# Filler matmuls on TensorE in a fused attention and expert-layer kernel: between the last four pair tiles, in the first six steps of the second attention pass, and in the prologue

## What is computed

```python
# layer 1: causal attention, 16 heads of 8 features, one shared key and value head
x = x + softmax(mask(q @ k.T / sqrt(8))) @ v @ w_proj      # q, k, v from layernorm(x) @ w_attn
# layer 2: experts picked by product keys, 8 heads, 16 experts each
xn = rmsnorm(layernorm(x)) * gamma
sim = (xn @ wq.T) . keys              # two lists of 32 key scores for each head
top 16 of sx[i] + sy[j], softmax over them
h = gelu(xn . table_down[idx]) * softmax(scores)
x = x + sum(h * table_up[idx])
```

## Time and profile before

| what | value |
|---|---|
| median of 3 runs | 1240.45 us (1239.9 to 1243.85) |
| the profiled execution | 1239.02 us |
| its span | 1237.2 us (1.8 us of the time lie outside the span) |
| mean granted TensorE clock | 0.763 |
| TensorE matmul, VectorE, ScalarE, GpSimd busy | 75%, 75%, 58%, 53% of the span |

### The profile page before, as it was taken

How to read it: one execution, slowest core, us unless ns; L and a number is a source line. 1 busy time by engine, 2 the same in 40 slices (tenths; PEclk the granted TensorE clock), 3 DMA queues, 4 the chain that set the end, 5 groups by cost and what they waited for, 6 DMA issues and landing times.

```text
span 1237.2 us, 21178 instructions
## 1 busy us (share of the span) xinstructions
PE 923.1 (75%) x5537; PEld 486.3 (39%) x5554; DVE 927.3 (75%) x4050; ACT 722.8 (58%) x1008; POOL 654.8 (53%) x371
## 2 busy tenths in 40 slices
PE   2784869687786968688796968778696877878544
PEld 1431425334343533434353443435344344534333
DVE  1325396987959597795959779595977959598997
ACT  1342574756657574665757466565756657574742
POOL 1100183764918276492927548292755829274843
PEclk9985766868778686877868686877868687777777
DMA  5211111020112102011110202011110201100000
GB/s 142 31 14 30 14 30 15 8 39 0 33 13 33 14 11 35 0 34 13 33 14 14 32 0 37 9 33 14 20 26 0 40 7 29 15 9 2 5 1 9
DMA packets 51537, 26.50 MB, mean 21 GB/s; under 512 B 5168, under 2 KB 51120, under 8 KB 51312
## 3 DMA queue, kind: packets, MB, share of 16 engines
q1 hardware_dynamic: 51504, 26.11, 12.9%
HBM read 19.93 MB, written 5.24 MB: 20 GB/s over the span
## 4 chain that ended last, share of the span: by engine, by line
PE 50%; DVE 30%; issue 9%; ACT 7%; DMA 2%; SPq 1%; DVEq 1%; POOL 0%; ACTq 0%; POOLq 0%
DVE prob L906 12%; PE score L1103 8%; PE misc L1123 7%; PE score L1073 6%; PE score L1105 5%; PE score L1076 5%; DVE late_scores L773 5%; PE score L1196 4%; ACT prob L636 4%; PE score L1153 3%; PE score L1184 3%; PE misc L1125 2%; PE misc L1163 2%; DVE cand_left L870 2%; ACT late_scores L540 2%
## 5 line engine op out<-in xcount | busy, mean ns | idle before, releaser
L445 POOL TENSOR_TENSOR acc<-acc,prob 128x1024 f32<-128x1024 f32 x186 | 441.2, 2372 | 16.6 <-DVE prob L906 0.5
L906 DVE SCALAR_TENSOR_TENSOR prob<-score,cut,prob 128x1024 f32<-128x1024 f32 x256 | 316.4, 1278 | 26.2 <-ACT prob L636 25.0
L636 ACT ACTIVATE prob<-score,neg_lse,unit 128x1024 f32<-128x1024 f32 x256 | 299.5, 1201 | 56.3 <-PE score L1184 37.3
L1184 PE MATMUL score<-sel,pieces_t 128*128 128x512 f16 x512 | 172.7, 433 | 121.4 <-DVE prob L906 119.1
L418 POOL TENSOR_TENSOR scale<-bounded,half_neg 128x2 f32<-128x2 f32 x16 | 11.2, 703 | 375.3 <-DVE bounded L817 375.3
L557 ACT ACTIVATE probs<-score 128x512 f32<-128x512 f32 x192 | 114.7, 597 | 140.6 <-PE score L1105 120.0
L1103 PE MATMUL score<-q_stack,k_stack 49*128 49x512 bf16 x192 | 110.8, 577 | 58.3 <-DVE prob L906 29.0
L788 DVE RECIPROCAL y_t<-misc 128x256 f32<-128x256 f32 x16 | 28.1, 1758 | 146.3 <-PE misc L1125 146.3
L540 ACT ACTIVATE late_scores<-score 128x512 bf16<-128x512 f32 x128 | 74.5, 597 | 104.9 <-PE score L1076 103.9
L1184 PEld LDWEIGHTS score<-sel,pieces_t 128*128 128x128 f16 x512 | 39.5, 103 | 213.5 <-DVE prob L906 187.1
L1073 PE MATMUL score<-k_ahead,q_ahead 48*128 48x256 bf16 (+1 forms) x512 | 96.0, 306 | 28.8 <-DMA q_ahead<-q_scratch 13.2
(11 more groups left out here) (111 smaller groups left out, 1556.9 us busy)
## 6 DMA issues: line engine op xcount, KB each, us to landing
q_ahead<-q_scratch SPq DMA_DIRECT2D x96, 64.0 KB
q_stack<-q_scratch SPq DMA_DIRECT2D x96, 64.0 KB
q_scratch<-qk_piece SPq DMA_DIRECT2D x16, 192.0 KB, 2.4
xin<-x SPq DMA_DIRECT2D x16, 128.0 KB, 4.5
xres<-x SPq DMA_DIRECT2D x16, 128.0 KB, 5.0
out<-fin SPq DMA_DIRECT2D x16, 128.0 KB, 5.5
k_ahead<-qk_piece SPq DMA_DIRECT2D x96, 4.0 KB
k_stack<-qk_piece SPq DMA_DIRECT2D x96, 4.0 KB
```

Of the source, the lines that this page charges most:

```text
L445: eng.tensor_tensor(acc[:, j, :], so_far, prob[:, j * FH + h, :], ALU.add).then_inc(acc_added, 1)
L636: eng.activation(prob[:, g, :], score[g % BUFS][:, :], ACT.Exp, bias=neg_lse[:, j, h:h + 1], scale=unit[:, :]).then_inc(prob_made, 1)
L906: eng.scalar_tensor_tensor(prob[:, g, :], score[g % BUFS][:, :], cut[:, j, h:h + 1], prob[:, g, :], ALU.is_ge, ALU.mult).then_inc(prob_mas ...
L1184: ins = eng.matmul(score[g % BUFS][:, cols], pieces_t[:, j, h, :], sel[:, cols], start=True, stop=True)
```

## The change

`keep_busy(bank, count)` issues `count` matmuls of the first 256 columns of `sel` with the identity `ident_h` as weights, into a PSUM bank whose contents nobody reads before they are overwritten. It is called

- after each of the last four pair tiles of iterations 0 to 13, 4 matmuls each into `misc0`;
- after each of the first six steps of the second attention pass, in iterations 0 to 14, 2 matmuls each into `misc0`;
- in the prologue, 40 matmuls into the first 256 columns of `score1` ahead of the first attention pass of batch 0, and 16 ahead of the norms of the weights.

Two waits for `max_t_made` stand ahead of the first two uses, so that ScalarE has read the row maxima out of `misc0`.

```diff
+            def keep_busy(bank, count):
+
+                for _ in range(count):
+                    eng.matmul(bank[:, 0:T], ident_h[:, :], sel[:, 0:T], start=True, stop=True)
+
...
                 eng.wait_ge(setup_dve, 3)
+                keep_busy(score[1], 40)
                 for u in range(MAX_STEPS):
                     scores_for_max(0, u)
...
                 max_transpose(0, v_next_made, 1)
+                keep_busy(score[1], 16)
                 eng.wait_ge(unit_step, 1)
...
                 if a:
+                    eng.wait_ge(max_t_made, every(max_t_made, i + 1))
                     for u in range(6):
                         scores_for_probs(i + 1, u)
+                        keep_busy(misc[0], 2)
...
+                if m:
+                    eng.wait_ge(max_t_made, every(max_t_made, i + 2))
                 if f:
                     for h in range(4, FH):
                         pair_scores(i, 1, h, a, m)
+                        if m:
+                            keep_busy(misc[0], 4)
```

## The result

The changed kernel takes 1190.28 us (median of four executions: 1186.66, 1188.38, 1192.18 and 1257.32), against 1240.76 us before. The ratio without the fourth is 0.9583, interval 0.9559 to 0.9606: 4.2% faster. I take the fourth for a second course of this kernel (another pattern into which the same program's iterations can fall) rather than a disturbance from outside; the experiments come back to it. The forecast was 1217 us: right in sign, less than half of the gain in size.

What follows compares the result with a forecast made beforehand. TensorE at 1.2 GHz was taken to bound each iteration's first half. Eight held passes at -4.7 us, seven lost at +2.2 and -1 for the prologue sum to -23.2: 1215.8 from the profiled 1239.0, 1217 as median; range 1165 to 1264.

Steps and rivals of the forecast that it cites:

- What bounds the kernel: TensorE, slow at 1.2 GHz, leads an iteration's first half; time taken from it there shortens the iteration, up to 12.3 us.
- The prices of fillers and steps: Filler 0.107 us high, 0.213 low; steps 0.75 or 1.29 us; pair-tile fillers free; a lost pass costs 2.2 us.
- How many passes are held: Of 14 second attention passes preceded by pair-tile fillers, 8 were taken to keep the high clock; no gain at five.
- or recoveries in the middle of a pass: Alternative to six to eleven held passes within the main forecast, together given chance 0.44 and 1192 to 1232 us.
- Together 4.7 us: Gain per held pass: first six steps 0.3, transposes 0.9, steps 6 to 11 2.8, first pass's six steps 0.7 us.
- the 8.3 us: Gain per pass if the clock stays high also through weighing of values, later transposes and hidden units: 4.7 + 1.9 + 1.7.
- I expect held and lost passes to alternate: A pass's changed length shifts the next against the chip's clock decisions, so passes would be mixed: 8 held, 7 lost.
- Rival 2: Wait for the last mask still costs the clock, fillers don't restore it: 1273 us, chance 0.14; in part 1245 to 1262, 0.12.
- Rival 1: Nearly every pass holds the high clock: 1176 us, chance 0.14; through the weighing too, about 1125 us, chance 0.04.
- Rival 3: Dense work in the pass regains the high clock by itself, fillers only take room: 1259 us, chance 0.03.
- rival 4: Held and lost passes pay for each other, five or so held: within 0.3% of 1240 us, chance 0.09.

Runs made afterwards that it cites:

- the bridge: Changed kernel plus eight fillers ahead of the first attention pass and one behind each of its steps 4 to 11; 1198.55 us.
- around_bridge: Changed kernel with eight of its twelve step fillers moved behind the first eight transposes, plus fillers ahead of and within the first attention pass; 1159.99 us.
- early fillers: Changed kernel with step fillers only behind steps 0 to 3, pair-tile and prologue fillers kept; 1238.22 us.
- 32-row fillers: Changed kernel with every filler on 32 of the array's 128 rows, same 256 columns; 1294.54 us.
- late_bridge: Changed kernel with step fillers only behind steps 4 and 5, plus eight fillers ahead of the first attention pass and one behind each of its steps 4 to 11; 1148.26 us.
- around: Changed kernel with eight of its twelve step fillers moved behind the first eight transposes; 1193.76 us.
- late_steps: Changed kernel with step fillers only behind steps 4 and 5, pair-tile and prologue fillers kept; 1189.63 us.

## Why the prediction was right in sign and short in size

**What bounds the kernel: right.** The time from the pass's start to L800 fell by 3.93 us and the iteration by 3.41.

**The prices of fillers and steps: right, but for one misread row.** High steps came at 0.75 us and low ones at 1.29, tiles still 1.19 apart, the wait for the last mask 1.67 for a reckoned 1.7. "The transposes are reached after 4.8 us" is misread: the rows say 609.62 to 614.24, 4.6. That makes the six held steps worth 0.1 us and not 0.3, and the forecast for a lost pass 2.5 and not 2.2; it was 1.9 (6.54 us to the transposes, not 7.1), since two steps were high and not one. The first pass of the prologue started at 28.5 and the second at 58.1, with the norms between them at 52.67 for 52.3: nothing won, where I had put 1 us.

**"How many passes are held": the step that failed.** I counted passes of two kinds, eight held at -4.7 us and seven lost at +2.2, alternating. In the trace only two of the fifteen are held from their start (iterations 1 and 14), one starts low and is lost (iteration 0), and twelve, iterations 2 to 13, are of a third kind: lost after 1.3 to 1.5 us and recovered at 8.1 to 8.3. Such a pass pays the 1.9 us of low steps, and has it back with 3.1 in steps 6 to 11 and more behind, net 3.41. I had the place of the gain and the reason (many-row work) but looked for it over the wait and not at the transposes; "or recoveries in the middle of a pass" stands in the forecast's bracket without a price.

**"Together 4.7 us": too small.** The held pass of iteration 1 reaches the weighing of values 15.3 us in for 21.1, 5.8 won, and L800 28.84 us in for 36.95, 8.1 won. The transposes and steps 6 to 11 won what was reckoned (0.9 and 3.1 for 0.9 and 2.8). The six steps of the first pass took 4.4 us where I had 5 to 5.5. And the clock was low for only 3.4 us, from 14.1, so that the work behind was faster too, which I had left at its old price. That is close to the 8.3 us that I gave only to a clock held right through.

By these rows the sum should have read: 11 iterations at 3.4, one at 8.1, and 5.1 and 3.9 at the end, less 3.5 and 0.6.

**"I expect held and lost passes to alternate": wrong for the changed kernel, right for others.** There the iterations settled at one length. Alternation came in the longer course of the step fillers (74.8, 72.0), with the bridge (65.3, 74.3) and with `around_bridge` (63.5, 66.4), neither of them quite regular, and a cycle of four with early fillers.

**Rival 2, the slower side.** Its first half is what happened in twelve passes: the clock falls soon after the wait for the last mask, even with the fillers before it. That the wait is the cause isn't shown, since iterations 1 and 14 hold the clock behind waits of 1.31 and 1.76 us. Its second half, no recovery, happened with the 32-row fillers (1294) and in the longer course (1257 in one execution of the changed kernel; 1267 to 1269 with step fillers). It gave 1273 us; the changed kernel took 1257 once, and 1187 to 1203 in the nine other executions.

**Rival 1** didn't happen: two passes were held, not fourteen. `late_bridge` comes nearest to its gain by another way, with the clock lost at 1.1 us, back at 7.9 and then high for 27.3: 64.86 us an iteration and 1148 us in all. **Rival 3** is ruled out by the 32-row run, whose dense passes stay low, and **rival 4** by a gain of at least 3.3%.

**What stays open.** Whether the eight transposes themselves help to bring the clock back or only the fillers next to them: no run took them apart. The Trainium skill, "TensorE: Matmul & The Clock Gate", section "Part 4: PE-mode transpose", says that they don't count like matmuls, and no run here shows it. One row points the other way: iteration 0 has the fillers but no first eight transposes (L1196), and its clock stays low for its first 27.6 us in the changed kernel and in `around`; but it also starts at a low clock, so this doesn't settle it. No execution of the changed kernel itself on its longer course was profiled; that its 1257 us are the course seen with step fillers alone is an inference from the like mean clock (0.742 and 0.744) and difference (69 us from the median of the other three, and 67 there; 58 without the prologue's fillers). And nothing here tells which start leads to which course, nor why iterations 1 and 14 hold the clock.

## What to carry to other kernels

When TensorE is dense and slow, read the granted clock by stretches, and then ask how many rows its matmuls use: filler matmuls over all 128 rows can buy back the clock, four of them in the right place (here right ahead of the transposes) did as much as twelve, and the same columns on few rows only cost time. In a loop, a gain in one iteration can be followed by a loss in the next (65.3 and 74.3 us), so judge by settled iterations and by the spread of executions, not by the best iteration.

## What the runs showed that I had not expected

- Where iterations settle at one length they hold it to 0.01 us or nearly, and the lengths seen are steps apart: 64.86, 68.27, 71.68 and 75.09 us, each 3.41 from the next. Four of the fourteen traces don't settle so. A saving within an iteration need not be seen: `late_steps` drops eight fillers of twelve and keeps 68.27. That savings short of the next length are lost in general is a guess from this one.
- One program, two times: 1201 and 1268 us with step fillers alone, in the same group on the same chip.
- TensorE busy for 27.30 of 27.30 us at half clock, with 21 fillers on 128 rows in that stretch (`bridge`, 311.60 to 338.90).
